# Vector work of the last chunk pairs moved over the block boundary, and down matmuls in another order, in a convolution + fp8-style FFN kernel

## What is computed

```
y = irfft(rfft(u) * rfft(K))[:L] + u * D;  y = y * mask
gate = fake_quant(y) @ gate_w.T;  up = fake_quant(y) @ up_w.T      # 512 -> 1376
hidden = silu(gate) * up
out = x + fake_quant(hidden) @ down_w.T                            # 1376 -> 512
```

## Time and profile before

| | |
|---|---|
| median of 3 runs | 330.37 us (330.34 to 330.87) |
| the profiled execution | 330.22 us |
| its span, first to last instruction | 328.1 us |
| busy: PE, DVE, ACT, POOL | 309.3, 303.1, 206.8, 14.7 us |
| granted TensorE clock | 1.000 (2.4 GHz) |

### The profile page before, as it was taken

The page is one execution under the profiler, slowest core; times in us unless marked ns, Lnnn a source line. Parts: engine busy times, 40 slices in busy tenths (PEclk is TensorE's granted clock), DMA queues, the critical chain, the costliest instruction groups (busy, mean ns, idle before and its releaser), DMA issues.

```text
span 328.1 us, 4875 instructions
## 1 busy us (share of the span) xinstructions
PE 309.3 (94%) x1591; PEld 162.5 (50%) x1591; DVE 303.1 (92%) x463; ACT 206.8 (63%) x316; POOL 14.7 (4%) x21
## 2 busy tenths in 40 slices
PE   0889899899999999999999999999999999989996
PEld 0557554445445544555455554555455454434444
DVE  6989999999998999989998999989999899997784
ACT  4748788467754958367763967466763968544540
POOL 4032000000001000010001000010001000010010
PEclk9999999999999999999999999999999999999999
DMA  6559999400002780066401690057401650070028
GB/s 241 104 170 227 249 283 375 185 1 2 0 0 28 156 332 2 0 113 246 153 0 16 130 364 1 0 102 235 177 0 12 134 242 0 0 130 0 0 34 224
DMA packets 13985, 38.27 MB, mean 117 GB/s; under 512 B 1456, under 2 KB 6672, under 8 KB 11024
## 3 DMA queue, kind: packets, MB, share of 16 engines
q1 hardware_dynamic: 8384, 26.48, 22.1%
q0 software_dynamic: 5584, 11.57, 20.3%
HBM read 33.80 MB, written 15.81 MB: 151 GB/s over the span
## 4 chain that ended last, share of the span: by engine, by line
PE 78%; DVE 16%; issue 2%; ACT 2%; DMA 1%; DVEq 0%; ACTq 0%
PE gate_ps L519 20%; PE up_ps L519 20%; PE down_ps L475 19%; PE y_ps L460 17%; DVE hq L835 2%; DVE hv L818 2%; DVE yt L791 2%; DVE yq L802 2%; DVE ht L826 2%; PE y_ps L560 1%; DVE ym L783 1%; PE down_ps L560 1%; DMA prm<-in_params 1%; DVE hq L843 1%; ACT sil L383 0%
## 5 line engine op out<-in xcount | busy, mean ns | idle before, releaser
L383 ACT ACTIVATE sil<-gate_ps,fac 128x512 f32<-128x512 f32 (+1 forms) x88 | 59.9, 682 | 85.3 <-PE gate_ps L519 84.4
L519 PE MATMUL gate_ps<-yq,wg 128*128 128x512 bf16 (+2 forms) x372 | 89.5, 363 | 3.8 <-DVE hv L818 2.5
L519 PE MATMUL up_ps<-yq,wu 128*128 128x512 bf16 (+2 forms) x372 | 89.5, 363 | 0.0
L460 PE MATMUL y_ps<-xt,toep 128*128 128x512 f32 (+3 forms) x256 | 80.6, 434 | 0.0
L475 PE MATMUL down_ps<-wd,hq 128*128 128x512 bf16 (+1 forms) x308 | 79.2, 379 | 0.9 <-DVE hq L843 0.9
L818 DVE SCALAR_TENSOR_TENSOR hv<-up_ps,fac,sil 128x512 f32<-128x512 f32 (+1 forms) x88 | 65.5, 744 | 13.3 <-ACT sil L383 11.2
L519 PEld LDWEIGHTS gate_ps<-yq,wg 128*128 128x128 bf16 x372 | 35.6, 100 | 45.4 <-issue 4.7
L460 PEld LDWEIGHTS y_ps<-xt,toep 128*128 128x128 f32 x256 | 47.1, 190 | 21.2 <-issue 2.4
L519 PEld LDWEIGHTS up_ps<-yq,wu 128*128 128x128 bf16 x372 | 36.3, 100 | 38.3
L826 DVE SCALAR_TENSOR_TENSOR ht<-hc,hv 128x1024 f32<-128x1024 f32 (+1 forms) x48 | 54.1, 1126 | 1.2 <-ACT hc L366 1.2
L835 DVE SCALAR_TENSOR_TENSOR hq<-hc,ht 128x1024 bf16<-128x1024 f32 (+1 forms) x48 | 54.0, 1125 | 0.0
(11 more groups left out here) (144 smaller groups left out, 122.8 us busy)
## 6 DMA issues: line engine op xcount, KB each, us to landing
xt<-in_xT SPq DMA_DIRECT2D x8, 1024.0 KB, 7.4
out<-in_x SPq DMA_DIRECT2D x7, 1024.0 KB, 5.9
out<-res POOLq DMA_DIRECT2D x7, 1024.0 KB, 7.9
toep<-kpad_scratch SPq DMA_DIRECT2D x6, 1024.0 KB, 9.9
toep<-kpad_scratch SPq DMA_DIRECT2D x7, 256.0 KB, 4.1
wd<-in_down POOLq DMA_DIRECT2D x1, 1280.0 KB, 22.0
xt<-in_x SPq DMA_DIRECT2D x1, 1024.0 KB, 7.7
out<-xt SPq DMA_DIRECT2D x3, 256.0 KB, 3.0
```

The source lines that it names most:

```text
L383: nc.scalar.activation(sil[b][0:w, :], gate_ps[b][0:w, :], ACT.Silu, scale=fac[0:w, S_GATE:S_GATE + 1]).then_inc(silu_done, 1)
L460: last = nc.tensor.matmul(y_ps[h % 2][:, d * P:L], toep[par][:, h, d * P:(d + 1) * P], xt[par][:, h, 0:L - d * P], start=(d == 0), stop=(d ...
L519: mm = nc.tensor.matmul(ps[b][0:w, cols], wt[:, k, c * P:c * P + w], yq[par][:, version, k, cols], start=(k == 0), stop=(k == LB - 1))
```

## The change

On DVE the rounding and the clip of pair 3 (`PAIRS - 3`) move from slots 9 and 10 to slot 0 of the following block: the rounding ahead of the product of chunk 0, the clip behind it. The rounding sum and rounding of pairs 5 and 4 and their clips move one slot on (slots 1 and 2). The mask of channel 0 moves from slot 9 to slot 0 of the next block. Block 5 keeps pair 3 in its own slots (`keep` False), so block 6 follows with the old places of pairs 4 and 5; block 6 hands pair 3 to block 7. On PE the down matmuls are taken by `DOWN_ORDER`: row tiles 0 and 1 with chunks 0 to 5, both again with chunks 6 to 10, then tiles 2 and 3 with all chunks. ACT copies tile 0 in slot 4 instead of 3. The instructions are the same and as many.

```diff
--- before.py
+++ after.py
@@ -465,8 +465,7 @@
 
             def down_part(g, par, c):
 
-                for s in range(HB * c, HB * (c + 1)):
-                    t, k = divmod(s, CH)
+                for t, k in DOWN_ORDER[HB * c:HB * (c + 1)]:
                     w = width(k)
                     if t == 0:
                         at_least(pe, hq_ready, PAIRS * g + k // 2 + 1)
@@ -850,44 +849,55 @@
                 v.scalar_tensor_tensor(xt[0][:, t, cols], ps[:, cols], f(S_DOWN), xt[0][:, t, cols],
                                        ALU.mult, ALU.add).then_inc(last_done, 1)
 
-            def slots(g, par, first, ahead):
+            def left_over(g, par, c, late):
+
+                last = PAIRS * g - 1
+                if late and c == 1 or not late and c == 0:
+                    rounded_sum(last, PAIRS - 1)
+                    rounded(last - 1, g - 1, 1 - par, PAIRS - 2)
+                    clip(last - 1, 1 - par, PAIRS - 2)
+                if late and c == 2 or not late and c == 1:
+                    rounded(last, g - 1, 1 - par, PAIRS - 1)
+                    clip(last, 1 - par, PAIRS - 1)
+
+            def slots(g, par, ahead, late, keep):
+                first = late is None
                 for c in range(CH):
                     n = CH * g + c
                     m = PAIRS * g + c // 2
+                    if late and c == 0:
+                        rounded(m - 3, g - 1, 1 - par, PAIRS - 3)
                     if first and c == 3:
                         rounded(m - 1, g, par, 0)
                     product(n, m, par, c)
                     if c % 2 == 0 and c:
                         rounded_sum(m - 1, c // 2 - 1)
-                    if c == 0 and not first:
-                        rounded_sum(m - 1, PAIRS - 1)
-                        rounded(m - 2, g - 1, 1 - par, PAIRS - 2)
-                    if c == 1 and not first:
-                        rounded(m - 1, g - 1, 1 - par, PAIRS - 1)
                     if first and c == 0:
                         mask_y(1, 1)
                     elif first and c == 1:
                         round_y(1, 1, 0)
                         clip_y(1, 1, 0)
-                    elif c in MASK_PLAN and MASK_PLAN[c][0] == 1 <= ahead:
-                        mask_y(g + MASK_PLAN[c][0], MASK_PLAN[c][1])
-                    if c == 1 and not first:
-                        clip(m - 2, 1 - par, PAIRS - 2)
-                        clip(m - 1, 1 - par, PAIRS - 1)
+                    elif ahead and c in MASK_PLAN:
+                        for h in MASK_PLAN[c]:
+                            mask_y(g + 1, h)
+                    if late and c == 0:
+                        clip(m - 3, 1 - par, PAIRS - 3)
+                    if not first:
+                        left_over(g, par, c, late)
                     if c % 2 and 1 < c < Y_FIRST and not (first and c == 3):
                         rounded(m - 1, g, par, c // 2 - 1)
                     if ahead and c in SUM_PLAN and not (first and SUM_PLAN[c] == 0):
                         sum_y(g + 1, SUM_PLAN[c])
-                    if c >= 4 and c % 2 == 0:
+                    if 4 <= c < Y_FIRST and c % 2 == 0:
                         clip(m - 2, par, c // 2 - 2)
                     if ahead and c in ROUND_PLAN and not (first and ROUND_PLAN[c] == 0):
                         round_y(g + 1, 1 - par, ROUND_PLAN[c])
                     if ahead and c in CLIP_PLAN and not (first and CLIP_PLAN[c] == 0):
                         clip_y(g + 1, 1 - par, CLIP_PLAN[c])
-                    if c == Y_FIRST:
-                        rounded(m - 1, g, par, c // 2 - 1)
-                    if c in MASK_PLAN and MASK_PLAN[c][0] == 2 <= ahead:
-                        mask_y(g + 2, MASK_PLAN[c][1])
+                    if not keep and c == Y_FIRST:
+                        rounded(m - 1, g, par, PAIRS - 3)
+                    if not keep and c == CH - 1:
+                        clip(m - 2, par, PAIRS - 3)
 
             mask_y(0, 0)
             dve.wait_ge(ym_done, 1)
@@ -911,15 +921,15 @@
             clip_y(0, 0, 3)
             sum_y(1, 0)
             dve.wait_ge(k_ready, 2 * len(K_GROUPS))
-            slots(0, 0, True, 2)
+            slots(0, 0, 2, None, True)
             for stored_k in k_stored:
                 dve.wait_ge(stored_k, 16)
             with dve.Fori(0, (NBLK - 4) // 2) as j:
-                slots(2 * j + 1, 1, False, 2)
-                slots(2 * j + 2, 0, False, 2)
-            slots(NBLK - 3, 1, False, 2)
-            slots(NBLK - 2, 0, False, 1)
-            slots(NBLK - 1, 1, False, 0)
+                slots(2 * j + 1, 1, 2, True, True)
+                slots(2 * j + 2, 0, 2, True, True)
+            slots(NBLK - 3, 1, 2, True, False)
+            slots(NBLK - 2, 0, 1, False, True)
+            slots(NBLK - 1, 1, 0, True, False)
             last = PAIRS * NBLK - 1
             rounded(last - 1, NBLK - 1, 1, PAIRS - 2)
             rounded_sum(last, PAIRS - 1)
@@ -938,14 +948,16 @@
     4: [(1, 3, [1, 3])], 5: [(1, 3, [2])],
 }
 
-MASK_PLAN = {9: (2, 0), 0: (1, 1), 3: (1, 2), 5: (1, 3)}
+MASK_PLAN = {0: (0, 1), 3: (2,), 5: (3,)}
 SCALE_PLAN = {0: (1, 0), 1: (1, 1), 4: (1, 2), 6: (1, 3)}
 MAGNITUDE_PLAN = {1: (1, 0), 2: (1, 1), 5: (1, 2), 7: (1, 3)}
 SUM_PLAN = {2: 0, 3: 1, 6: 2, 8: 3}
 ROUND_PLAN = {3: 0, 4: 1, 7: 2, 9: 3}
 CLIP_PLAN = {3: 0, 4: 1, 7: 2, 9: 3}
 Y_FIRST = 9
-OUT_SLOTS = [3, 6, 9, 10]
+OUT_SLOTS = [4, 6, 9, 10]
+DOWN_ORDER = [(t, k) for tiles, chunks in (((0, 1), range(6)), ((0, 1), range(6, CH)), ((2, 3), range(CH)))
+              for t in tiles for k in chunks]
 LAST_PARTS = [(0, 0, slice(0, L)), (1, 0, slice(0, L)), (2, 0, slice(0, L)),
               (HB - 1, 0, slice(0, L // 2)), (HB - 1, 1, slice(L // 2, L))]
 
```

## The result

The changed kernel takes 334.96 us (median of 4 runs, 334.86 to 335.36) against 330.36 us before (4 runs, 330.24 to 330.87): ratio 1.0139, 95% interval 1.0121 to 1.0156. It is 4.6 us slower. The profiled execution took 334.86 us with a span of 333.2, 5.1 more than before. The forecast was 334.9, from +4.55.

A forecast was written before the change was run, and what follows sets the result against it. PE was taken to bound blocks 1 to most of 6, DVE two short places. Block 1 +0.66, blocks 2 to 4 +3.72, block 5 +1.05, blocks 6 and 7 −0.88 make +4.55: 334.9 us, range 332.0 to 336.5.

The forecast's parts named there:

- The bound: PE bounds from block 1 to most of block 6; DVE around the block 0/1 and block 6/7 boundaries.
- (a), the bank wait: Slot 1's convolution piece on PE waits 0.65 us for the moved mask of channel 0, which reads its bank.
- (a), ACT 1.11 later: ACT's scaling of channel 0 waits for the moved mask and starts 1.11 us later, as does chunk 2's SiLU.
- (b): Moved pair work on DVE, with the late mask, delays chunk 5's product; PE starts chunk 7 1.24 us later per block.
- Block 1, +0.66: In block 1 product 5 comes later, and the gate matmuls of 88.22 start at 88.88: 0.66 us lost.
- Block 5, +1.05: In block 5, outside the loop, product 5 comes later and the matmuls of 236.82 move to 237.87: 1.05 us lost.
- Blocks 6 and 7, −0.88: DVE-bound end: the mask delays block 6, then block 7's waits shrink; chunk 4's gate matmuls start 0.88 us earlier.
- (c): New down matmul order on PE, tile 0 copied in slot 4: cost 0, and it lets the pairs move.
- A: Rival: only the bank wait at the convolution piece counts, +1.7, 332.1 us; chance 0.08.
- B: Rival: the mask is in time, blocks 1 to 6 cost nothing, the kernel is faster at 327.7 us; chance 0.06.
- C: Rival: hand-overs from mask to ACT and product to PE cost 0.26 more together in five blocks, 336.2 us; chance 0.16.
- D: Rival: masks and roundings don't bind and no stage was bound by DVE, so no change; chance 0.02.

The follow-up runs named there:

- e5: The changed kernel with the convolution piece that waits for the mask (channel 2, first distance) moved from slot 1 to slot 2 on PE; 335.72 us.
- e2: The kernel before with only the new order of the down matmuls and tile 0 copied in slot 4; 329.49 us, ratio 0.9963.
- e3: The kernel before with only the mask of channel 0 moved from slot 9 to slot 0, right behind the product of chunk 0; 334.39 us.

## Why the prediction was right, point by point

- *The bound.* Right. No engine got another instruction and the kernel is slower. The page's shares went down (94 to 93%, 92 to 91%).
- *(a), the bank wait, 0.65.* Right in size: 0.66 by starts. Its parts were not. The piece starts 0.06 after the mask's end (147.07 to 147.13), not 0.15, but its two matmuls take 0.96 us (147.13 to 148.09) and not 0.86. The rows of the weight loads show the first of them at 147.13, with the matmul; before it was at 144.17, 0.22 ahead of it.
- *(a), ACT 1.11 later.* Right, and 0.08 too small: the hand-over from mask to ACT is 0.12 (147.07 to 147.19), where I took 0.04 from another wait. It is 0.11 to 0.12 in blocks 1 to 4 and 0.03 in blocks 5 and 6 (223.83 to 223.86); why is not shown.
- *(b), 1.24 per block.* 1.32, 1.32 and 1.31 in blocks 2 to 4, the difference being those 0.08. The 0.92 of pair 5 is in the rows: 155.16 − 154.24. That the bank wait lies inside the 1.24 is shown by e5.
- *The rule of the Trainium skill*, "VectorE: DVE Perf Modes", The DRAIN you can't avoid, that a semaphore wait between two vector operations adds nothing, does not hold in this place: the clip of pair 5 starts 0.71 after its rounding (154.24 to 154.95), while a 96x512 instruction with no such wait behind it, pair 5's sum, takes 0.60 (149.79 to 150.39 by starts, in the same trace). The same rounding took 0.60 in the kernel before, where pair 4's clip came behind it. The measurement decides.
- *Block 1, +0.66:* 0.75. *Block 5, +1.05:* 1.06 (5.88 − 4.82). *Blocks 6 and 7, −0.88:* −0.85 (5.03 − 5.88). The sum is 4.92 in the trace against 4.55, and 4.60 by the medians. (Three chunks of 2.59 from 288.95 end at 296.72, not at the 296.75 that the prediction has, a slip of 0.03.) So 0.37 was missing from the sum, 0.23 of it in blocks 2 to 4, and that the median comes within 0.1 us of the forecast is partly luck.
- *(c), the down order at cost 0.* This was the step that failed. The order is worth −1.04 us (e2), all of it in block 7. The prediction lets the wait before 294.16 go in the sum of blocks 6 and 7 but prices the order at 0, and e2's expectation of 330.4 says the same. The sum of these blocks came out right only because both edits are in it. I asked what the mask and the pairs remove, and not what the down matmuls themselves no longer wait for, though they are what waited there. That the new order is needed for the moved pairs, as (c) says, no run shows: none moves the pairs under the old order.
- *The rivals.* A (the bank wait alone) falls in the change, which waits at chunk 7; e3 is the kernel in which A holds. B was right on what it would take: with the mask in time the kernel is faster. C's direction was right at 0.08 per block, not 0.26. D falls with the 4.6 us.

## What to carry to other kernels

When two engines are nearly full, moving an instruction between slots can be as good as free for its own engine and still cost on the others: look at who waits for its result, how much work is queued behind that waiting instruction, and how much slack the next product has. Put an instruction that others wait for in front of its engine's own idle time, not behind the instruction that ends it; here that exchange was worth 6.3 us. And price each edit of a change alone, since a wait that disappears belongs to the edit that the waiting instruction needs; the sum can be right with the terms in the wrong place.

## What I had not expected

Two waits of the bound engine in one block, each of 0.66 us, and removing the first gave nothing (e5): the time at which a late producer delivers decided, not the number of waits. A convolution piece that waits for its bank takes 0.10 us more for two matmuls than one that doesn't (0.96 against 0.86 by starts). And the ten kernels' profiled executions differ by up to 1.1 us before block 1 is reached (61.12 to 62.21 for the same matmuls), as much as some of the effects; the stretch from block 0 to the tail leaves it out.
